# Another written-out order of the items of every engine in an AdaLN attention layer on one core

## The reference

```python
x = x + attn(moe(x, cond))       # moe: 8 experts of 64 units, the top 2 of a softmax over logits, and shared experts
                                 # attn: q k^T / sqrt(128*32), a band of 32 below the diagonal, times v, layer norm
x = x + ffn(attn2(x, cond))      # attn2: norm, 16 heads of 64 with normed q, one k and v for all heads, a null key,
                                 # relative position bias from a small MLP, causal softmax, output projection, norm
                                 # ffn: silu(x w1) * (x w2), gelu(h1), gelu(h2), w3
```

## Time and profile before

| | us |
|---|---|
| median of 3 runs | 814.14 (812.65 to 814.35) |
| profiled execution, first to last instruction | 811.5 |
| PE busy | 777.8 (96%) |
| ACT busy | 602.6 (74%) |
| DVE busy | 581.3 (72%) |
| POOL busy | 460.3 (57%) |

### The profile page before, as it was taken

One profiled execution on the slowest core, in us unless ns is written; L12 is line 12 of the kernel. 1 busy time (PEld: TensorE's weight loads), 2 busy tenths in 40 slices (PEclk: granted clock), 3 DMA queues, 4 the chain that ended last, 5 costly groups with the idle time before them and its releaser, 6 DMA issues.

```text
span 811.5 us, 16623 instructions
## 1 busy us (share of the span) xinstructions
PE 777.8 (96%) x5322; PEld 593.4 (73%) x5322; DVE 581.3 (72%) x1575; ACT 602.6 (74%) x1647; POOL 460.3 (57%) x388
## 2 busy tenths in 40 slices
...
DMA packets 28917, 23.41 MB, mean 29 GB/s; under 512 B 2192, under 2 KB 26400, under 8 KB 28448
## 3 DMA queue, kind: packets, MB, share of 16 engines
...
q10 hardware_dynamic: 304, 0.01, 0.0%
...
## 4 chain that ended last, share of the span: by engine, by line
PE 68%; DVE 13%; POOL 7%; issue 5%; ACT 1%; DVEq 0%; POOLq 0%; ACTq 0%
PE ps_M L1243 33%; PE ps_S L1369 6%; PE ps_T L1384 6%; PE ps_z L1397 5%; PE ps_T L1377 5%; DVE sb_sm L1131 5%; PE ps_M L1429 3%; PE ps_M L1296 3%; POOL sb_sm L660 2%; PE ps_S L1351 2%; POOL sb_biasm L653 2%; DVE sb_hT L1043 2%; POOL sb_rq L643 1%; PE ps_M L1326 1%; DVE sb_bs L1033 1%
## 5 line engine op out<-in xcount | busy, mean ns | idle before, releaser
L660 POOL TENSOR_TENSOR sb_sm<-sb_sm,sb_rden 128x512 f32<-128x512 f32 x128 | 146.2, 1145 | 155.6 <-DVE sb_rden L1144 155.6
L759 ACT ACTIVATE sb_sm<-sb_sm,sb_nmx 128x129 f32<-128x129 f32 x512 | 200.1, 397 | 28.4 <-DVE sb_nmx L1139 28.0
L653 POOL TENSOR_TENSOR sb_biasm<-sb_bias,sb_maskn 128x512 f32<-128x512 f32 x128 | 168.8, 1326 | 57.3 <-DVE sb_sm L1131 36.7
L1131 DVE SCALAR_TENSOR_TENSOR sb_sm<-ps_S,sb_rq,sb_biasm 128x129 f32<-128x129 f32 x512 | 141.0, 345 | 24.0 <-PE ps_S L1369 20.1
L643 POOL TENSOR_TENSOR sb_rq<-sb_qss,sb_mhalf 128x16 f32<-128x16 f32 x32 | 93.2, 2938 | 21.9 <-DVE sb_qss L1116 21.9
L759 ACT ACTIVATION_READ_ACCUMULATOR sb_sm<-sb_sm,sb_nmx 128x1 f32 x512 | 99.1, 193 | 0.0
L1369 PEld LDWEIGHTS ps_S<-sb_k,sb_qs 64*128 64x128 f32 x1024 | 65.2, 187 | 40.7 <-issue 38.4
L773 ACT ACTIVATE sb_pT<-ps_T 128x512 f32<-128x512 f32 x128 | 74.8, 593 | 26.8 <-PE ps_T L1377 26.8
L1139 DVE TENSOR_REDUCE sb_nmx<-sb_sm 128x4 f32<-128x516 f32 x128 | 86.2, 682 | 1.4
L1369 PE MATMUL ps_S<-sb_k,sb_qs 64*128 64x129 f32 x1024 | 83.0, 291 | 3.8 <-DVE sb_sm L1131 2.2
L1377 PE MATMUL ps_T<-sb_ident,sb_sm 128*128 128x128 f32 x512 | 77.1, 276 | 3.7 <-POOL sb_sm L660 3.5
...
## 6 DMA issues: line engine op xcount, KB each, us to landing
...
sb_xg<-in_xT SPq DMA_DIRECT2D x8, 256.0 KB, 4.1
sb_xs<-in_x SPq DMA_DIRECT2D x8, 256.0 KB, 4.6
...
out_y<-sb_res SPq DMA_DIRECT2D x7, 256.0 KB, 3.9
...
```

The costliest lines, as they stand in the source:

```text
L653: pool.tensor_tensor(biasm[:, heads, 1:NK], bias0[:, heads], maskn[:, j // 4].unsqueeze(1).broadcast_to([128, 4, S]), ALU.add)\
L660: pool.tensor_tensor(sm[:, heads, 1:NK], sm[:, heads, 1:NK], rden[:, heads].unsqueeze(2).broadcast_to([128, 4, S]), ALU.mult)\
L759: ins = act.activation(sm[:, h], sm[:, h], ACT.Exp, bias=nmx[:, h:h + 1], accum_out=den[:, h:h + 1])
L1131: ins = dve.scalar_tensor_tensor(sm[:, h], bank(g, "sim", n, odd)[:, m * NK:(m + 1) * NK], rq[:, k * HEADS + h:k * HEADS + h + 1], biasm[: ...
```

## The change

The table `ORDER` has new texts for all phases of PE, ACT, DVE and POOL but the drain of PE, DVE and POOL, and for SP's fill and steady. Each text holds the same items as before, but for the deal of the 22 `warm`. The functions are the same, but for two waits on DVE that the new order needs. Buffers and the numbers of banks are as they were; which bank an item gets follows from PE's list. The line numbers of the changed kernel are two lower up to DVE's `null_key`, one lower from there to `rw_take`, and equal behind it. Its core:

```diff
     "act steady": """
-        xh.0 exp.0-3 ex.0 exp.4 ex.1-2 down.0 zT.0 ex.3 qkv.0 PT.0 l1.0 PT.1 l1.1 h1.0 PT.2 h1.1 l1.2-3 PT.3
+        xh.0 exp.0-4 ex.0-1 down.0 zT.0 ex.2 qkv.0 ex.3 l1.0-1 PT.0-1 h1.0 l1.2 h1.1 PT.2-3 l1.3 h1.2 PV.0 h1.3
...
     "pool fill": """
-        pb.0 nb.0 pb.1 nk.0 ln1.0 xb.0 ln2.0 bias+.0-2 kv.0 bias+.3 qn.0-3
+        xb.0 pb.0-1 ln1.0 ln2.0 nk.0 nb.0 bias+.0-2 kv.0 bias+.3 qn.0-3
...
             def null_key(g, k):
                 if k == 0:
+                    dve.wait_ge(load["rows"], 16)
                     link(dve.tensor_tensor(nks, nkey_r, nkey_r, ALU.mult), null_sum)
...
             def rw_take(g, k):
                 dve.wait_ge(rw_psum.sem, rw_psum.at(g, 0))
+                dve.wait_ge(routed, (g + 1) * ROUTE_OPS)
                 dve.tensor_copy(rg[:, 0:GB * 2 * E],
```

More of the change, by code:

```diff
@@ L58 @@
+        kv.0 qs.0-3 q.4-7 qs.4-7 warm.19 qst.0 kT.0 warm.20-21
     """,
     "pe start": """
[L60 to L63, removed]
+        rw.0 sim.0 exp.0-1 sim.1 exp.2 sim.2 exp.3 PT.0 sim.3 PT.1 exp.4 PT.2 sim.4 down.0 PT.3 sim.5 PV.0 qkv.0
@@ L70 @@
+        q.6-7 z.5 qs.4-7 PT.13-14 kT.0 PT.15 qst.0 PV.6-7 z.6-7
     """,
     "pe seventh": """
[L72 to L75, removed]
+        sim.0 exp.0-1 sim.1 exp.2-3 sim.2 exp.4 down.0 zT.0 PT.0-1 sim.3 qkv.0 l1.0 sim.4 l1.1 PT.2 l1.2-3
@@ L82 @@
+        PT.15 PV.6-7 z.6 l2d.3 z.7 l3d.0-1
     """,
@@ L100 @@
+        PT.13-15 kT.0 PV.6-7
     """,
     "act seventh": """
[L102 to L105, removed]
+        xh.0 exp.0-4 ex.0-2 down.0 zT.0 ex.3 qkv.0 PT.0-1 l1.0-1 h1.0-1 l1.2 PT.2 l1.3 ex.4 h1.2-3 ex.5 PT.3
@@ L119 @@
-        q.4-5 kT.0 ssq.0 vs.0 ssc.0 q.6-7
+        cg.0 pb.0 rt.0 pb.1 rt.1 x0.0 rt.2 wl.0 rt.3-4 rw.0 pl.0 exp.0 pb.2 exp.1 rt.5 exp.2 nk.0 exp.3 pb.3
+        exp.4 rt.6-7 xl.0 down.0 rt.8 qkv.0 scores.0 pl.1 mix.0 rt.9 ln1.0 pl.2 ln2.0 maskn.0 pl.3 xnT.0 q.0-3
+        kv.0 q.4 nk.1 q.5 kT.0 ssq.0 ssc.0 q.6 vs.0 q.7
     """,
     "dve start": """
-        xl.0 rw.0 sim.0 max.0 exp.0 sim.1 inv.0 max.1 exp.1 sim.2 inv.1 exp.2 max.2 exp.3 inv.2 max.3 sim.3
-        max.4 inv.3 exp.4 sim.4 max.5 inv.4 pl.4 down.0 max.6 inv.5 sim.5 max.7 qkv.0 scores.0 inv.6 sim.6 inv.7
@@ L124 @@
-        max.8 mix.0 sim.7 inv.8 max.9 ln1.0 max.10 inv.9 sim.8 max.11 ln2.0 inv.10 sim.9 inv.11 max.12 xnT.0
-        sim.10 inv.12 maskn.0 max.13 kv.0 q.0 max.14 sim.11 inv.13 max.15 inv.14 q.1-2 pl.5 q.3-4 inv.15 kT.0
-        q.5-6 ssq.0 ssc.0 vs.0 q.7
+        rw.0 xl.0 sim.0 exp.0 max.0 exp.1 sim.1 max.1 inv.0 exp.2 sim.2 max.2 inv.1 max.3 exp.3 inv.2 sim.3
+        exp.4 inv.3 max.4 sim.4 pl.4 max.5 down.0 sim.5 inv.4 max.6-7 inv.5-6 qkv.0 scores.0 sim.6 inv.7 max.8
+        sim.7 mix.0 max.9-10 inv.8 sim.8 inv.9 ln1.0 max.11 inv.10 sim.9 ln2.0 max.12 sim.10 xnT.0 inv.11
```

104 lines of the change are left out of this document (52 added, 52 removed).

## The result

| | before | after |
|---|---|---|
| median, us | 813.57 (812.65 to 814.35, 4 runs) | 820.45 (818.50 to 822.41, 4 runs) |
| ratio | | 1.0086, 95% interval 1.0067 to 1.0105 |
| profiled execution, span | 811.5 | 816.7 |

A forecast was written before the change was run, and what follows sets the result against it. TensorE, busy 96% of the span, was taken as the bound. Steady terms of +1.55 us, five times +7.75, with fill -1.3 and other stages 0, gave +6.45 on 814.14: 820.6 us, 8 in 10 between 810 and 829.

The forecast's parts named there:

- (a): Steady iteration, `down`: its wait for a bank held by VectorE's share of `exp.3` goes, -0.45 us.
- (b): Steady iteration, `l1.1`: ACT's `ex.3` now precedes the silu, so TensorE's second half waits, +0.75 us (bounds 0 and 1.6).
- (c): Steady iteration: VectorE waits for the silu before `sim.3`; the slip reaches `sim.5` and `l2.0`, +0.6 us (bounds 0 and 1.2).
- (d): Steady iteration, `l3.0`: VectorE's `ln1` between `h2.1` and `h2.2` makes TensorE wait, +0.7 us (bounds 0 and 1.6).
- faster* rival: VectorE and ACT run ahead over the whole steady iteration, removing four new waits: 806.6 us, chance 0.20.
- (e): Steady iteration, `xnT`: earlier `ln1` has the norm ready long before, so the wait goes, -0.7 us.
- (f): Steady iteration: `ex.10-11` and table loads before ACT's `l3.1` delay `PT.10`, `PT.11` and `l4`, +0.75 us (bounds 0 and 1.5).
- (g): Steady iteration, TensorE: changes from full to part tiles rise from 11 to 15, costing 0.1 each, +0.4 us.
- (h): Steady iteration: half to two thirds of seven small waits among `q` items go, with `q` in pairs, -0.5 us.
- Fill: Fill: `xb.0` first delays VectorE's `pb.1`, but later `rt.8-9` bring `qn` forward, -1.3 us (bounds -3 and +2).
- The table load: ACT's silu: the trace shows no extra 1.38 us drain per switch; the skill's rule gives 827.5 us, chance 0.02.
- much slower rival: `bias` items before `pn` on GpSimd hold up `PT` and the next `sim`: 831 us, chance 0.10.

## Why the prediction was right in its total and wrong in its parts

The items of one steady iteration, as the time from each start on TensorE to the next, summed by kind, tell the terms apart (before 93.2, after 92.5). The recorded sign of being wrong was a period at or under 93.2: by it the mechanism was wrong in steady, though the total came out.

- (a) `down` without its wait, -0.45: **right**. The `exp` items with it took 8.03 and take 7.38, and `down` starts 0.23 behind the last matmul of `exp.4`.
- (b) `l1.1` waits for the silu, +0.75: **right**. `l1` went from 5.99 to 6.78.
- (c) `sim.5` and `l2.0`, +0.6: **absent**. `l2` takes 11.47 and `sim` 9.54 in both. VectorE made up the slip: `h1.3` ends at 275.12, 0.7 before the fourth quarter of `l2.0`.
- (d) `l3.0` behind `ln1`, +0.7: **absent**, `l3` went from 11.64 to 11.54. This is the step that failed most plainly: "`h2.3` between 291.3 and 292.3" rested on the 5.16 us of the old `ln1`. Measured, `ln1` takes 4.1 and `h2.3` ends at 295.90, 0.3 to 0.4 before the fourth quarter of `l3.0`, which began at 294.08. `ln1` itself began 47.7 us into the iteration, where the walk had it (47.6 to 48.5). Had it taken its old time, `h2.3` would have come, by an estimate from these rows, 0.7 too late for that quarter, which is the term as forecast. So the failed step is the duration that was taken over, and not the order of the items. The *faster* rival named this point as the one that decides, and its head start was there too: `qn` begins 3.4 us before the next `sim.0`, where it began 1.4 before.
- (e) `xnT` without its wait, -0.7: **right**.
- (f) exps between the gelus, +0.75: **absent**; `PT.10`, `PT.11` and `l4` wait for nothing.
- (g) tile changes, +0.4: `PV` -0.41, `z` +0.27 and `PT` (without the wait of (e)) +0.27, so about +0.1.
- (h) `q` items, -0.5: 6.33 to 6.01, -0.3.

The sum is -0.7 where I had +1.55: (a), (b) and (e) came as forecast, (h) nearly, and of the four terms that rest on VectorE or ACT being late, (b), (c), (d) and (f), only (b) came.

- **Fill**, -1.3: the steps of `xb` and of `pb.1` at 13.5 (measured 14.03) were right; "`down`'s split near 38.6, `ln1` near 48.8, `qn` at 70.7" came at 40.08, 50.49 and 73.39. The walk priced TensorE's items at full clock, and had no price for `lg.1-5` in front of `rw.0`.
- **Start and seventh**, 0 each: "`kv` 4 later, end even" left out SyncE's queue behind `pl.5`, though the step was moved past it, and had no price for a lower clock (0.98 in the stage, 1.8 us); "`l3.0` waits 1 for `h2.3`" was seen and came true (0.8 and 0.4), but was set off against a gain that did not come.
- **The table load**: ACT's first silu of the iteration again starts right behind its load (the load ends at 263.68, the silu starts at 263.70), as the rows had it; nothing of a further 1.38 us shows.

- **The much slower rival** put its +2.8 an iteration down as the bounds of all terms. The upper bounds add up to +4.65, and taken half way to +3.1; no wait on `pn` appeared in steady.

The forecast's number was right because the losses of fill, start and seventh, and what the new phases cost each other, stood in for a loss in steady that was a gain. That is luck: the steady lists have the opposite sign from the forecast, in the changed kernel and alone.
